# Attention and quantized FFN on one core: start-up loads, the first matmuls of the last batch, and the order around the hand-over to the FFN

## The reference, cut to what matters

```python
# x (8, 100, 2048), ctx_4096 (8, 722, 2048), all float32; qweight (2048, 1536) int32
def xattn(query, key):                      # keys are the values too, no scaling
    e = softmax(einsum('bqd,bkd->bqk', query, key), axis=-1)
    return einsum('bqk,bkd->bqd', e, key)
def ffn(x, qweight, scale, zero_point, bias):
    w = (unpack6(qweight) - zero_point) * scale      # four 6-bit values in three words
    return einsum('bsk,nk->bsn', x, w) + bias
x = x + tanh(g_xattn[0]) * xattn(layernorm(x), ctx_4096)
x = x + tanh(g_ffn[0]) * ffn(layernorm(x), qweight, scale, zero_point, bias)
```

## Time and profile before

| what | value |
|---|---|
| median of 3 runs | 592.06 us (589.16 to 598.02) |
| the profiled execution | 585.18 us |
| its span, first to last instruction | 583.3 us |
| granted clock of PE, mean | 0.999 |
| PE busy | 569.0 us |
| DVE, ACT, POOL busy | 358.9, 287.7, 217.0 us |

### The profile page before, as it was taken

The page is one execution under the profiler, slowest core; times in us unless marked ns, Lnnn a source line. Parts: engine busy times, 40 slices in busy tenths (PEclk is TensorE's granted clock), DMA queues, the critical chain, the costliest instruction groups (busy, mean ns, idle before and its releaser), DMA issues.

```text
span 583.3 us, 8789 instructions
## 1 busy us (share of the span) xinstructions
PE 569.0 (98%) x3454; PEld 409.8 (70%) x3454; DVE 358.9 (62%) x684; ACT 287.7 (49%) x451; POOL 217.0 (37%) x196
## 2 busy tenths in 40 slices
PE   7979999999999999999999999989999999999997
PEld 6969969968968968978977986555564444444445
DVE  6667717827836836745755764694859764654443
ACT  3756566568567666676675757354232220210000
POOL 3037177169259349439439519711000000000000
PEclk9999999999999999999999999999999999999999
DMA  8999649236947848738848668669756984872311
GB/s 247 296 299 242 193 160 319 66 104 225 228 144 249 225 108 298 224 98 261 265 104 281 193 161 366 225 111 284 233 183 187 252 237 134 194 152 66 89 55 40
DMA packets 44436, 113.69 MB, mean 195 GB/s; under 512 B 21027, under 2 KB 21283, under 8 KB 35779
## 3 DMA queue, kind: packets, MB, share of 16 engines
q1 hardware_dynamic: 27168, 107.71, 60.7%
q10 hardware_dynamic: 16970, 5.42, 5.2%
q0 software_dynamic: 256, 0.00, 0.0%
HBM read 89.26 MB, written 19.66 MB: 187 GB/s over the span
## 4 chain that ended last, share of the span: by engine, by line
PE 79%; DVE 7%; DMA 5%; POOL 3%; SPq 3%; issue 1%; ACT 1%
PE S L1164 18%; PE S L1056 12%; PE T L1010 8%; PE pv L1164 8%; PE S L1058 7%; PE pv L1094 6%; PE S L1094 6%; PE pv L1010 5%; POOL vlo L495 3%; DMA xa<-in_x 3%; DVE xres L783 3%; PE pv L1105 2%; PE S L1105 2%; DMA raw<-in_L_ffn_qweight 2%; SPq L330 2%
## 5 line engine op out<-in xcount | busy, mean ns | idle before, releaser
L495 POOL TENSOR_TENSOR vlo<-raw,vhi 128x2048 fp32r<-128x2048 f32 (+1 forms) x38 | 174.1, 4606 | 50.3 <-ACT vhi L563 50.3
L1056 PE MATMUL S<-khi,qT 128*100 128x362 f32 x512 | 141.3, 357 | 0.0
L1058 PE MATMUL S<-klo,qT 128*100 128x362 f32 x256 | 85.3, 333 | 3.5 <-DVE klo L912 3.0
L912 DVE TENSOR_TENSOR klo<-pv,khi 128x361 fp32r<-128x361 f32 x128 | 65.3, 527 | 23.6 <-ACT khi L552 23.0
L912 DVE TENSOR_TENSOR klo<-T,khi 128x361 fp32r<-128x361 f32 x128 | 65.7, 529 | 21.5 <-ACT khi L552 20.6
L563 ACT ACTIVATE vhi<-raw 128x2048 fp32r<-128x2048 f32 (+1 forms) x38 | 72.0, 1911 | 6.3 <-PE S L1094 6.2
L552 ACT ACTIVATE khi<-T 128x361 fp32r<-128x361 f32 x128 | 58.4, 475 | 33.0 <-PE T L1010 32.8
L1164 PE MATMUL S<-raw 128*128 128x512 f16 x320 | 71.7, 379 | 1.6 <-issue 1.6
L552 ACT ACTIVATE khi<-pv 128x361 fp32r<-128x361 f32 x128 | 58.6, 476 | 29.8 <-PE pv L1010 29.8
L1056 PEld LDWEIGHTS S<-khi,qT 128*100 128x100 f32 x512 | 67.9, 167 | 0.0
L1010 PE MATMUL T<-ident,raw 128*128 128x128 f32 (+1 forms) x416 | 64.0, 268 | 0.4 <-DVE qT L902 0.3
(11 more groups left out here) (128 smaller groups left out, 748.6 us busy)
## 6 DMA issues: line engine op xcount, KB each, us to landing
raw<-in_ctx SPq DMA_DIRECT2D x24, 1024.0 KB, 10.4
raw<-in_L_ffn_qweight SPq DMA_DIRECT2D x16, 768.0 KB, 7.7
raw<-in_ctx SPq DMA_DIRECT2D x12, 840.0 KB, 9.0
raw<-in_ctx SPq DMA_DIRECT2D x32, 256.0 KB, 10.2
xres<-in_x SPq DMA_DIRECT2D x8, 800.0 KB
x_scratch<-xres SPq DMA_DIRECT2D x8, 800.0 KB
rows_scratch<-xres SPq DMA_DIRECT2D x8, 800.0 KB
late<-x_scratch SPq DMA_DIRECT2D x24, 256.0 KB, 4.8
```

What stands on the lines that cost most here:

```text
L495: pool.tensor_tensor(vlo[0:r, k, :], raw[0:r, b % 2, t, :], vhi[0:r, k, :].bitcast(F32), ALU.subtract).then_inc(s_vlo, 1)
L912: dve.tensor_tensor(klo[:, slot, 0:GW], T[k][:, 0:GW], khi[:, slot, 0:GW].bitcast(F32), ALU.subtract).then_inc(s_free[k], 1)
L1056: pe.matmul(into[0:R, g, 0:MW], qT[:, h, c, :], khi[:, slot, :], start=(c == 0 and h == 0), stop=False)
L1058: last = pe.matmul(into[0:R, g, 0:MW], qT[:, 0, c, :], klo[:, slot, :], start=False, stop=(c == CH - 1))
```

## The change

Eight edits, none of which changes what is computed:

- PE, last batch: `LAST_ORDER` becomes `[3, 0, 5, 1, 4, 2]`. Float32 tile 3 comes first and clears the accumulators, so the wait on `s_x1` moves to it; split tile 2 comes last.
- PE, hand-over: in `attend(6)` `probs(7)` moves between the two halves of `normed(0)`; in `attend(7)` every inserted piece moves one tile earlier, and `weights(3)` moves from behind `attend(7)` to before its last tile. The bank order follows.
- SP, start: the pieces of contexts 0 and 1 become 512, 512 and 1024 columns for group 0, 1024 and 1024 for group 1 (15 loads each in place of 24); `next_x(1)` moves before the last piece of context 0; all four pieces of the first x are issued by SP.
- DVE, ACT and PE, start: the statistics of x of batch 1 begin a step earlier (21 for 22); ACT's splits of context 0 move to steps 17, 24, and for tile 2 to step 13 of the next batch; PE turns the queries of batch 1 at steps 32 and 34 of `scores(0)` and after it.
- SP, hand-over: `x1_out(6)` goes before `next_xres(7)`; `rows_out(6)` behind `load_rows(3)` and `load_w(5)`; `load_w(6)` behind `x1_out(7)` and the first two `load_x1`.
- ACT, hand-over: `probs(7)` and then `ln2_norm(5)` move before the second half of `rows_hi(0)`; `weights(2)` before `ln2_norm(6)`.
- DVE, hand-over: `probs_lo(7)` moves between the halves of `rows_lo(0)`, `unpack(3)` between those of block 1; `residual(7)` goes before `unpack(4)`, and `rows_lo(2, 0)` before `ln2_stats(7)`.
- ACT: the wait on `s_pv` in `probs` is left out for batch 7, whose copy goes to `E` and not to `ph`.

```diff
-    LAST_ORDER = [0, 1, 5, 3, 2, 4]
+    LAST_ORDER = [3, 0, 5, 1, 4, 2]
...
+        PIECES = [[(0, 1), (1, 1), (2, 2)], [(0, 2), (2, 2)]]
...
-                fill("x", 0, 4)
+                fill("x", 0, 2)
                 fill("P", LAST, 2)
+                fill("x", 0, 2, 2)
...
-            for c in (0, 2):
+            for c in range(NCH):
                 sp.dma_start(xa[0:R, piece(c)], x[0, :, piece(c)]).then_inc(s_xa0[c], 16)
             def context_pieces(b):
                 for g in range(2):
-                    for c in range(NCH):
+                    for c, n in PIECES[g]:
+                        if (b, g, c) == (0, 1, 2):
+                            next_x(1)
+                        cols = slice(c * 512, (c + n) * 512)
...
             context_pieces(0)
-            next_x(1)
...
             rows_out(LAST - 2)
+            x1_out(LAST - 1)
             next_xres(LAST)
-            x1_out(LAST - 1)
             used(LAST, 2)
             load_rows(2)
             load_w(RT)
-            rows_out(LAST - 1)
             load_rows(3)
             load_w(RT + 1)
+            rows_out(LAST - 1)
             load_rows(4)
-            load_w(RT + 2)
             x1_out(LAST)
             for j in range(2):
                 load_x1(j)
+            load_w(RT + 2)
...
-                if b >= 1:
+                if 1 <= b < LAST:
                     act.wait_ge(s_pv, b * NCH)
...
-            for c in (1, 3):
-                act.dma_start(xa[0:R, c * 512:(c + 1) * 512], x[0, :, c * 512:(c + 1) * 512]).then_inc(s_xa0[c], 16)
             queries(0)
-            keys_hi(0, {17: lambda: context_hi(0, 0), 22: lambda: context_hi(0, 1), 27: lambda: context_hi(0, 2)})
+            keys_hi(0, {17: lambda: context_hi(0, 0), 24: lambda: context_hi(0, 1)})
...
+                    between[13] = lambda: context_hi(0, 2)
...
                     rows_hi(0, 0)
+                    probs(LAST)
+                    ln2_norm(i - 1)
                     rows_hi(0, 1)
-                    ln2_norm(i - 1)
                 context_hi(i + 1, 1)
-            probs(LAST)
...
+            weights(2)
             ln2_norm(LAST - 1)
-            weights(2)
...
-            hooks = pieces_of(1, 22, 2)
+            hooks = pieces_of(1, 21, 2)
...
             rows_lo(0, 0)
+            probs_lo(LAST)
             rows_lo(0, 1)
             residual(LAST - 1)
-            probs_lo(LAST)
             ln2_stats(LAST - 1)
             unpack(2)
             rows_lo(1, 0)
+            unpack(3)
             rows_lo(1, 1)
             scale_and_bias()
-            unpack(3)
+            residual(LAST)
             unpack(RT)
-            residual(LAST)
+            rows_lo(2, 0)
             ln2_stats(LAST)
-            rows_lo(2, 0)
...
-                        if b < 2 and c % 4 == 0:
+                        if b < 2 and c % 4 == 0 and any(c == 4 * begin for begin, n in PIECES[g]):
...
+                            if first:
+                                pe.wait_ge(s_x1, (b - 1) * NCH + n + 1)
                             last = pe.matmul(pv[n][0:R, :], p, raw[0:r, b % 2, t, n * 512:(n + 1) * 512],
-                                             start=False, stop=final)
+                                             start=first, stop=final)
...
-            scores(0)
-            queries(1)
+            scores(0, {2 * CH: lambda: queries(1, (0, 1)), 2 * CH + 2: lambda: queries(1, (2,))})
+            queries(1, (3,))
...
-                    attend(i, {3: lambda: normed(0, (0, 1)), 4: lambda: normed(0, (2, 3)), 5: lambda: probs(LAST)})
-            attend(LAST, {1: lambda: weights(0), 2: lambda: weights(1), 3: lambda: normed(1, (0, 1)),
-                          4: lambda: normed(1, (2, 3)), 5: lambda: weights(2)})
-            weights(3)
+                    attend(i, {3: lambda: normed(0, (0, 1)), 4: lambda: probs(LAST), 5: lambda: normed(0, (2, 3))})
+            attend(LAST, {0: lambda: weights(0), 1: lambda: weights(1), 2: lambda: normed(1, (0, 1)),
+                          3: lambda: normed(1, (2, 3)), 4: lambda: weights(2), 5: lambda: weights(3)})
```

More of the change, by code:

```diff
@@ L327, in context_pieces @@
                 for g in range(2):
-                    for c in range(NCH):
+                    for c, n in PIECES[g]:
+                        if (b, g, c) == (0, 1, 2):
+                            next_x(1)
+                        cols = slice(c * 512, (c + n) * 512)
                         for t in range(3 * g, 3 * g + 3):
-                            sp.dma_start(raw[0:ROWS[t], b, t, piece(c)],
-                                         ctx_in[b, FIRST[t]:FIRST[t] + ROWS[t], piece(c)]).then_inc(s_first[b][g][c], 16)
+                            sp.dma_start(raw[0:ROWS[t], b, t, cols],
+                                         ctx_in[b, FIRST[t]:FIRST[t] + ROWS[t], cols]).then_inc(s_first[b][g][c], 16)
             context_pieces(0)
-            next_x(1)
             for k, g in enumerate((g_xattn, g_ffn)):
```

## The result

| what | before | changed |
|---|---|---|
| median of 22 runs each | 589.05 us (584.88 to 600.88) | 598.8 us (593.52 to 613.86) |
| ratio, with its 95% interval | | 1.0175 [1.015, 1.02] |
| the profiled execution | 585.18 us | 607.51 us |
| its span | 583.3 us | 605.7 us |

The change makes the kernel slower: 1.0175 times 589.05 is 10.3 us more, with an interval of 8.8 to 11.8 us, where a gain of 3.9 us was forecast.

What follows compares the result with a forecast made beforehand. PE was taken as the bound (busy 569.0 of 583.3 us), leaving only its idle time to win. Start 1.6 plus hand-over 2.3 (2.7 + 0.6 - 1.0) gave 3.9 us: execution 581.3, median 588, range 581 to 595.

Steps and rivals of the forecast that it cites:

- Start, T = 31.0, 1.6 us won: Start: a wait for context replaces PE's wait for DVE; batch 1 starts at 41.2, 1.6 us won, ends -1.3 and +3.3.
- T: Start: time at which context 0's last piece lands; PE starts batch 1 at the later of T + 10.15 and 39.5.
- Slower by larger pieces: Rival, start: 1024-column pieces move at 225 GB/s, T is 38.0, batch 1 starts 5.4 us late; result 595, chance 0.08.
- turning point: Start: the T from which the larger pieces make the kernel slower, given as 35.2, a rate of about 260 GB/s.
- Hand-over, three waits removed, 2.7 us: `attend(7)`: PE's waits for `vlo` at tiles 0 and 1 and for ACT's `weights(3)` copies go: 0.40 + 0.66 + 1.63.
- "After attend(7)", 1.0 us charged, ends of 0 and 3.3: After `attend(7)`: earlier `load_w(5)` wins 0.6 us; late `load_w(6)` and chains behind `ln2_norm(7)` charged 1.0, ends 0 and 3.3.
- the worst case: After `attend(7)`: `load_w(6)` issued near 398 lands at 411, `rows_lo(4, 0)` behind it, PE loses 2.8 us.
- Both gains are given back: Rival, start and hand-over: T = 33.9 and `load_w(6)` late, 1.3 us lost, 0.5 won, about 593; chance 0.14.
- The one on the slower side: Rival, start: larger pieces at 225 GB/s start batch 1 5.4 us late; result 595, chance 0.08.
- The 0.90: Whole kernel: chance that the result lies within about 2%, 11.8 us, of the kernel before; 0.07 faster, 0.03 slower.

Runs made afterwards that it cites:

- e4: Kernel before with only the change's start edits (larger context pieces, second x, first x, queries, statistics, splits); ratio 1.0000 to the kernel before.
- e1: The changed kernel run again, unaltered; ratio 1.0152 to the kernel before.
- e3: Kernel before with one move alone, `load_w(6)` behind the first two `load_x1`; ratio 1.0109 to the kernel before.
- e13: Changed kernel with only DVE's order edited, `unpack(6)` behind both halves of block 4, `load_w(6)` still late; ratio 1.0018 to the kernel before.
- e6: Changed kernel with `rows_out(6)` put back ahead of `load_rows(3)` and `load_w(5)`, `load_w(6)` left late; ratio 1.0188 to the kernel before.
- e2: Changed kernel with only `load_w(6)` put back ahead of `x1_out(7)`; ratio 1.0033 to the kernel before.
- e5: Changed kernel with `load_w(6)` still earlier, right behind `rows_out(6)` and ahead of `load_rows(4)`; ratio 1.0017 to the kernel before.
- e9: Changed kernel with `load_w(6)` between `x1_out(7)` and the two `load_x1`; ratio 1.0149 to the kernel before.
- e10: Changed kernel with the two `load_x1` first, then `load_w(6)`, then `x1_out(7)`; no ratio, 597.0 us (4 runs) beside 588.6.
- e17: Changed kernel with old start, `rows_out(6)` and `load_w(6)` put back, `unpack(6)` behind block 4, `ln2_stats(7)` right behind `residual(7)`; ratio 1.0042 to the kernel before.

## Why the prediction was wrong

Point by point, by its own steps. Its base was also high: 592.06 us was the median of three runs, and over 22 it is 589.05.

- *Start, T = 31.0, 1.6 us won.* In the first profile T is 31.30 and batch 1 begins at 41.13 where 41.2 was forecast. That is luck: 31.30 is the earliest of the fourteen profiles with the new start, where T runs from 31.30 to 35.38 with a median of 33.2, and the 42.79 that it was compared with is the earliest of the five with the old one. Over ten runs the start alone is worth 1.0000 [0.9965, 1.0034], that is -2.0 to +2.1 us. The mechanism was right (a wait for data replaces the one for DVE, and step 8 waits too); the size is not distinguishable from zero. By the rule of the Trainium skill that was weighed there (DMA: Bandwidth & Descriptors, on the semaphore's 16 and on queues and rings), T would be no better than 31.7; thirteen of the fourteen profiles agree, and the first, with 31.30, is 0.4 us better.
- *Slower by larger pieces.* Its T of 38.0 did not come, nor did e4 show any loss: the large pieces cost nothing that can be told. (Its turning point is T = 34.9 by the prediction's own terms, 42.79 + 2.3 - 10.15, not 35.2; nothing hangs on it.)
- *Hand-over, three waits removed, 2.7 us.* Right: 3.0 us in each pair of profiles. No wait on `s_x1` at tile 3, none on `vlo`, block 1 in time. `load_rows(3)` and `load_w(5)` were issued at 374.58 and 375.25, and the 2.40 us of the earlier trace rows are gone in this profile; in seven others with the same order of these loads DVE still waited 0.7 to 2.1 us.
- *"After attend(7)", 1.0 us charged, ends of 0 and 3.3.* This step failed. The issue was foretold well (near 398; it was 397.80), and so was the path: `rows_lo(4, 0)` behind `unpack(6)`, PE waiting for a bank. Wrong was the landing: 13.0 us, the row of the load in its old place, was used for a load that the change puts behind a store of 800 KB and two more loads. In its new place it took 16.5 to 18.1 us (changed, e1, e3, e13) and 23.9 in e6, and the wait was 8.6 us where the worst case had 2.8. Undoing it gave back 8.4 us (e2), and moving the consumer aside 9.2 us (e13).
- *The same step, a second omission.* A wait was priced at its length. In this kernel the clock fell in it and stayed low behind it, which cost another 1.4 us by the rows at 418.25 and 419.90; over all runs the mean clocks only bound such costs, at 6.0 us, and no run separates them.
- *And a third.* The prediction names the chain behind `ln2_norm(7)` (it "doesn't come earlier, while PE does") but prices it inside the same 1.0 us, and not the wait at `weights(4)` that it makes: 1.5 to 4.7 us with SP's order as changed (changed, e1, e2, e5, e9, e10, e13). Where the store is put back the wait is 1.6 to 4.1 us, behind the late `load_w(5)`. Either is of the size of the hand-over's gain.
- *The rivals.* "Both gains are given back" named `load_w(6)` and had it at 593, 0.14; it was the nearest to what happened. The one on the slower side looked for the cause at the start, where it wasn't. No case had more than 3.3 us for these chains; the range ended at 595, set by the slower case at the start, and 598.8 lies outside it. The 0.90 for a result within 2% of the kernel before came true, with a loss of 1.75% in place of a gain.

What stays open: what sets the time of the load exactly. The same 768 KB took 7.5 to 13.6 us in nine profiles when issued after 394 us ahead of the x1 store (14.8 and 19.4 when issued at 390 to 392, 16.2 in e17), and 13.1 to 18.1 behind the store or the loads of x1; e6 took 23.9. Behind them it landed between 414 and 420 us whether issued at 391 or at 404, which suggests waiting for other traffic, the store first of all, but no run separates the queue from the memory.

## What to carry to other kernels

Price a DMA that is moved back in a queue by what will then be ahead of it, not by its time in the old place, and walk through everything that stands behind its consumer on that engine: in e13 the same late load cost nothing that could be told once its unpack had been moved behind two others. When PE is made to arrive earlier, subtract that from the slack of every later chain that doesn't come earlier too, most of all those through DRAM; in this kernel the 3.0 us won before the first product came back as waits for a bank or a block each time. A term that is under 1% and rests on one arrival in one execution should be forecast as zero, with its spread as the range.

## What was not expected of the hardware

The same load of 768 KB took between 7.5 and 23.9 us to land, and behind the 800 KB store of x1 even 2.5 KB took 14.6 to 21.5 us; it took 6.6 to 17.4 us from the issue of the store of the rows of batch 6 until the load that waits for it could go. The weights that a DMA transposes and that PE takes at 511 us arrived up to 11.4 us late in some executions of kernels whose order there is the same, and not at all late in others. The granted clock was lower where PE had waited some microseconds: 0.86 in the window 400 to 450 us of e1 with waits of 3.4 and 7.6 us, 0.93 in the changed kernel with 1.5 and 8.6, and 1.00 in e2 with 2.8 and 0.2:

```profile
400.00:450.00 50.00, 39.00 (x219) 22.84 (x218) 23.49 (x38) 15.06 (x22) 0.86 (x2) 0.86 0.68 177
```

```profile
400.00:450.00 50.00, 47.88 (x313) 26.98 (x314) 35.51 (x59) 17.57 (x26) 0.86 (x2) 1.00 0.74 220
```

The first is e1, the second e2 (columns as in the window above). The Trainium skill, TensorE: Matmul & The Clock Gate, says in the section "What's actually happening" that the clock is set by how busy the engine has been recently; these rows agree.
